# Small extra matmuls on TensorE after every step of the attention phase

## The reference

```
z   = q k^T / 8                              # per head, 2048 x 2048
lom = where(mask, -softplus(z), 0)           # mask: strictly lower triangle
s   = reverse_cumsum(lom, over keys) - lom
att = where(mask, exp(log_sigmoid(z) + s), 0)
o   = att v
x   = x + (o Wo^T) + moe_ffn(xn)             # 32 low-rank experts and a shared one
```

## Time and profile before

| | us |
|---|---|
| median of 3 runs (lowest, highest) | 8487.61 (8464.02, 8512.73) |
| the profiled execution: time | 8526.3 |
| its span, from the first to the last instruction (core 4, the slowest) | 8524.8 |
| spans of the 8 cores | 8405.2 to 8524.8 |
| mean granted TensorE clock of core 4 | 0.716 |
| PE busy, share of the span | 5427.3, 64% |
| DVE busy | 3253.1, 38% |
| ACT busy | 2889.5, 34% |
| weight loads of PE busy | 1589.4, 19% |

### The profile page before, as it was taken

How to read it: one execution, slowest core, us unless ns; L and a number is a source line. 1 busy time by engine, 2 the same in 40 slices (tenths; PEclk the granted TensorE clock), 3 DMA queues, 4 the chain that set the end, 5 groups by cost and what they waited for, 6 DMA issues and landing times.

```text
span 8524.8 us, 81563 instructions; the slowest of 8 cores (8405.2 to 8524.8 us)
## 1 busy us (share of the span) xinstructions
PE 5427.3 (64%) x17588; PEld 1589.4 (19%) x17588; DVE 3253.1 (38%) x5812; ACT 2889.5 (34%) x4306; POOL 854.9 (10%) x1617
## 2 busy tenths in 40 slices
PE   2223556677776777777677656377667757766775
PEld 0011111122211222222112112112222121222212
DVE  7211224344444444444444411166236506623650
ACT  0000334344444444444444500044125404512440
POOL 0101111110001111000010000100110010001001
PEclk9866655666655666666556578688888888878878
DMA  2001547510000000000000034311341161134116
GB/s 75 12 4 10 64 46 89 66 12 7 6 6 7 8 8 8 6 6 6 6 8 1 0 64 100 72 55 62 104 121 52 46 182 55 62 92 125 55 39 170
DMA packets 222122, 408.82 MB, mean 48 GB/s; under 512 B 141576, under 2 KB 144032, under 8 KB 215760
## 3 DMA queue, kind: packets, MB, share of 16 engines
q0 software_dynamic: 200592, 353.00, 19.5%
q1 hardware_dynamic: 20784, 50.47, 2.5%
q10 hardware_dynamic: 272, 0.14, 0.0%
HBM read 451.83 MB, written 85.07 MB: 63 GB/s over the span
## 4 chain that ended last, share of the span: by engine, by line
PE 45%; DMA 18%; DVE 13%; ACT 11%; issue 10%; another core or an unknown queue 2%; DVEq 1%; ACTq 0%; SPq 0%; POOL 0%; POOLq 0%
PE pbq L510 7%; PE zp L639 5%; PE zp L645 5%; DMA cd<-scr_cd 5%; ACT att L565 4%; DMA xp<-x 4%; PE pboA L579 4%; DVE gu L821 4%; PE zp L548 3%; DVE lsb L651 3%; PE pboB L579 2%; ACT g L813 2%; DMA wv<-WvT 2%; PE pbL L810 2%
## 5 line engine op out<-in xcount | busy, mean ns | idle before, releaser
L651 DVE TENSOR_TENSOR lsb<-zp,z 1x512 bf16<-1x512 f32 (+3 forms) x1152 | 668.7, 589 | 1324.8 <-PE zp L645 1309.1
L579 PE MATMUL pboA<-att,vtok 128*64 128x512 bf16 (+2 forms) x640 | 347.0, 542 | 885.8 <-ACT att L565 738.1
L606 ACT ACTIVATE texp<-zp 128x1024 bf16<-128x1024 f32 x448 | 458.8, 1024 | 912.8 <-PE zp L548 737.8
L565 ACT ACTIVATE att<-zp 128x1024 bf16<-128x1024 f32 x448 | 458.4, 1023 | 671.6 <-DVE lsb L651 432.3
L639 PE MATMUL zp<-sp,tri 128*128 128x512 bf16 (+3 forms) x1280 | 642.1, 508 | 55.6 <-DVE z L626 48.9
L626 DVE COPY z<-zp 1x512 f32<-1x512 f32 (+3 forms) x1152 | 623.9, 577 | 0.6 <-issue 0.2
L645 PE MATMUL zp<-lsb,ones 1*128 1x512 bf16 (+2 forms) x1152 | 611.0, 530 | 0.0
L821 DVE TENSOR_TENSOR gu<-g,pbL 128x512 bf16<-128x512 bf16 x704 | 484.1, 688 | 192.0 <-PE pboA L817 64.4
L821 DVE TENSOR_TENSOR gu<-g,zp 128x512 bf16<-128x512 bf16 x704 | 484.2, 688 | 169.8 <-PE zp L817 57.9
L793 ACT ACTIVATE zg<-zp 128x512 bf16<-128x512 f32 x64 | 38.2, 597 | 1488.2 <-PE zp L790 1488.2
L813 ACT ACTIVATE g<-zp 128x512 bf16<-128x512 f32 x704 | 420.6, 597 | 279.4 <-PE zp L807 204.3
(11 more groups left out here) (186 smaller groups left out, 6930.0 us busy)
## 6 DMA issues: line engine op xcount, KB each, us to landing
cd<-scr_cd POOLq DMA_DIRECT2D x256, 512.0 KB, 4.8
cgu<-scr_cgu POOLq DMA_DIRECT2D x136, 704.0 KB, 4.5
scr_cgu<-CguT POOLq DMA_DIRECT2D x32, 704.0 KB, 77.6
x<-x SPq DMA_DIRECT2D x16, 1024.0 KB, 4.8
scr_cd<-CdT POOLq DMA_DIRECT2D x32, 512.0 KB, 79.3
xp<-x SPq DMA_DIRECT2D x64, 256.0 KB, 4.8
out<-op SPq DMA_DIRECT2D x64, 256.0 KB, 3.0
out<-yst POOLq DMA_DIRECT2D x16, 1024.0 KB, 8.0
```

The lines of the kernel that those rows point to most:

```text
L565: Sc.op("ACT", lambda sc, zp=zp: sc.activation(t_att[zp][:], zpair_ap[zp][:], AF.Exp), reads=[pr[(0 if zp == 0 else 6)], pr[(0 if zp == 0 ...
L579: Sc.op("PE", lambda t, zp=zp, pjb=pjb, p0=p0, oc0=oc0, first=first, po=po, hs=hs: t.matmul(pbank[po][0:64, oc0:QT], t_vtok[:, pjb * 128 + ...
L651: Sc.op("DVE", lambda v, zp=zp, h0=h0, c0=c0, hs=hs: v.tensor_tensor(t_lsb[hs][:, c0:QT], zpair_ap[zp][0:1, h0 + c0:h0 + QT], t_z0[hs][:, ...
```

## The change

After every step of `gen_headpair`, and before the unit of `gen_qkv` that may follow it, PE issues three extra matmuls. Each multiplies a 64x64 corner of the constant tile tri with itself (64 rows, 64 weight columns, 64 moving columns) and writes the result to a corner of bank 4. Nobody reads it. The three are recorded as writers of bank 4, so the first of them is given a wait on whoever still reads that bank. It is 3 x 1984 = 5952 matmuls, each with its weight load; nothing is removed or moved.

```diff
@@ -21,6 +21,7 @@
 ATTN_HPS = None
+HEAT_N = 3
@@ -665,6 +666,13 @@
                     reads=[pr[po]], writes=[res("oF")])
             yield
 
+    def heat(n):
+        for _ in range(n):
+            Sc.op("PE", lambda t: t.matmul(
+                pbank[4][0:64, 0:64], t_tri[0:64, 0:64], t_tri[0:64, 0:64],
+                start=True, stop=True),
+                reads=[res("tri")], writes=[pr[4]])
+
     hps = list(range(NHC)) if ATTN_HPS is None else list(ATTN_HPS)
@@ -674,6 +682,7 @@
         for _ in gen_headpair(hp):
             step += 1
+            heat(HEAT_N)
             if nxt is not None and step % 2 == 0:
                 try:
                     next(nxt)
```

## The result

The changed kernel takes 8679.42 us (median of 10 runs, 8668.1 to 8753.28) against 8490.01 us (10 runs, 8447.14 to 8532.12). The ratio is 1.0236, with a 95% interval of 1.0203 to 1.027: slower by 2.4%. (The ratio is worked out over the runs; the quotient of the two medians is 1.0223.) The forecast was 8805 us, 3.7% slower, in a range of 8600 to 9060.

The account below looks back on a forecast made before the run. A serial ring of 5.77 us per key block in pure attention, at clock 0.50, bounds the kernel. 20.3 us for each of 15 pairs plus 12 us for the last make +316 us: 8805 us, range 8600 to 9060.

Parts of the forecast that it names:

- the ring: One key block's serial chain in pure attention, through PE, DVE, ACT and back to PE: 5.77 us, forecast about 6.1.
- the hole: PE's idle 2.05 us per key block, between the last L645 and the next pboA; forecast to shrink to about 1.4.
- (a): Groups after steps C and A, without projections: 0.66 us in PE's idle 2.05 us, so they cost nothing.
- (b): Groups after step B, without projections, on the serial chain: 30 x 0.33 = 9.9 us a pair (4.8 to 19.8).
- (c): Groups during projection units, where PE is full: 24 x 0.24 = 5.8 us a pair (1.9 to 11.5).
- L555's step: Nearest matmul, 128 weight and 128 moving columns: 0.22 us at clock 0.50, 0.16 at 1.00; half priced one extra matmul.
- (d): First extra matmul after a unit waits for DVE's evacuation of bank 4; with transposes 4.6 us a pair (4.1 to 5.5).
- (e): PE's clock: given nothing; the level stays at 0.50 in pure attention.
- R1: Rival: the fill brings the clock back in pure attention; -300 us, about 8190 us; chance 0.09.
- R2: Rival: no change, the group after step B vanishes too; time about 8520 us; chance 0.05.
- R3: Rival: waits on bank 4 drop the clock in the projection stage too; 96 us more, 8900 us; chance 0.08.
- the same length as before from the output projection on: Sign expected in the profile: everything from the output projection to the end keeps its length, no gain or loss.

Follow-up runs that it names:

- k12_after: The changed kernel run once more, unaltered; ratio 1.0239 (1.0164 to 1.0315) to the kernel before, attention 4331 us.
- k3_only_ac: The changed kernel with the three extra matmuls only after steps A and C, none after B; ratio 1.0108 to the kernel before, attention 4166 us.
- k0_before: The kernel before the change, run once more unaltered for a second profile; ratio 1.0025 (0.9989 to 1.0062), attention 4077 us.
- k1_bank2: The changed kernel with the extra matmuls writing bank 2, unused in attention, instead of bank 4; ratio 1.0193 to the kernel before, attention 4268 us.
- k10_dense6: Against the changed kernel: six full 128-row matmuls into bank 2, only after step C outside projection units; ratio 0.9489 to the kernel before.
- k4_dense4: Against the changed kernel: four full 128-row matmuls into bank 2, only after step C outside projection units; ratio 0.9594 to the kernel before.
- k6_dense4_64: Like the kernel with four full matmuls after step C, but on 64 rows instead of 128; ratio 1.0095 to the kernel before.

## Why the prediction was right, and where its sizes were off

The direction, the place and the mechanism held: serial work on the ring, nothing in the hole, a new wait on bank 4, no change of the clock. The sum was too large: 316 us forecast, 189 measured between the medians (222 between those of k12_after's runs and of the kernel before beside them, 8684.56 and 8462.33). Two things made it so: attention grew by 253 us and not by 316, and a later stage became shorter.

(a) Groups in the hole cost nothing: shown (the ring of k3_only_ac is 5.76 us, its last pair as long as that of k0_before).

(b) A group on the ring was put at 0.33 us (0.16 to 0.66): it is 0.29. (c) One at the fast clock at 0.24: it is 0.18 to 0.21. This pair of rows of the changed kernel at clock 1.00 shows a wait first, then the group, 3396.22 - 3396.04 = 0.18 us to the next start:

```profile
3396.04 0.25 PE L671 MATMUL pbq<-tri 64*64 64x64 bf16 x3 [0.50 <-DVE q L521]
3396.22 0.39 PE L640 MATMUL zp<-sp,tri 128*128 128x512 bf16 x1
```

Half of L555's step was a good price, a little high. With 0.29 and 0.20 the sum becomes 30 x 0.29 + 24 x 0.20 + 4.6 = 18.1 us a pair, 282 with the last, against 253 to 254 measured in attention. The comparison block by block says where the other 30 us are. Without the waits a pair grew by 12.1 us (k1_bank2) and not by 13.5; the waits add 4.1 and not 4.6; the last pair grew by 8.8 and not by 36 x 0.29 = 10.4. The term that is off is (c): the seven blocks with projection units grew by 2.5 to 3.1 us a pair in k1_bank2 (against k0_before and the first profile), not by 24 x 0.20 = 4.8. (c) had PE full there, and it wasn't throughout: in the block that closes the first query block PE waits 1.46 us a pair for att before the change and 0.74 us after it (core 4), so groups ran in idle time there too.

(d) The wait was forecast as 4.1 us a pair for the projection units, 62 us, and the trace has 31.3 + 16.9 + 14.1 = 62.3 us. That the two agree is luck. I had four waits of 1.02 us a pair, 60 in all, and none otherwise. The trace has three a pair directly behind a unit, 45 of 0.94 us, which are 42.4 us; the fourth unit after a C step is followed by the closing step with its product with v. The other 19.9 us are 60 shorter waits of 0.20 to 0.75 us that I had called hidden, such as the 0.50 above, in a block with no scores matmul behind the unit. The transposes wait 17.5 us, where I took 7.5 and a bound of 21. k1_bank2 gives back 63 to 72 us when it is gone.

(e) The clock stayed at 0.50 in pure attention and at 1.00 with projections, and R1 fell. R1's price was of the right kind: k10_dense6 has a ring of 4.29 us where I had said 5.77 - 1.5 = 4.3; what brought the clock was more work, on all rows. The rule of the Trainium skill, "TensorE: Matmul & The Clock Gate", section "What's actually happening", that activity releases the throttle, agrees with k4_dense4 (0.82) and is too coarse for k6_dense4_64, where PE is busy 95% of the time at 0.50. R2 is out by the same rows as (b). R3 came in a small way: of 176 projection units on each core (those after the first 900 us), 21 to 26 take over 0.26 us a matmul, a sign of the low level, against 20 or 21 before. At most six units of about 3 us each are under 20 us a core.

The term that was wrong is one that I set to nothing, "the same length as before from the output projection on". The output projection became 27 us shorter from k0_before to k12_after (329 to 302) and 54 shorter than in the profile that I had read (362 to 308). 253 - 54 = 199 us between the medians of the cores, near the 189 measured, and 254 - 27 = 227 for the repeats, near their 222. The total would lie in the range without this gain too; the gain only took it further from 8805. A gain there was in no part of my sum and in no rival.

## What to carry to other kernels

Filler matmuls must be priced by where they stand in the chain: six in a hole of 2 us were free, three on the ring cost their full 0.29 us, and a shared bank turned the harmless ones into waits of up to 0.9 us. If filler is to lift the clock, watch PEclk and not PE's busy time, put it into the hole, give it all 128 rows and an unused bank, and try several amounts: here two full matmuls did nothing, four won 4%, six 5%, and eight no more than six. Compare the stages that a change doesn't touch too, and take the profile of the unchanged kernel twice.

## What the runs showed of the hardware

- Four matmuls of 512 columns on 64 rows kept PE busy 189.72 of 200 us and the granted clock stayed 0.50; the same four on 128 rows brought it to 0.82 on average.
- A matmul with 64 weight columns and 64 moving ones, repeated, starts about every 0.06 us at clock 0.50 (six last 0.53 us and three 0.36 or 0.37, so about 0.17 for three more); the group of three costs 0.29 us in the list, more than three steps of 0.06, so entering and leaving the group costs about 0.1 us more. Whether that is the other tile shape or the weight load was not tried.
- The output projection, identical code, took 299 to 310 us in the changed kernel and 320 us or more in the kernel before, on all cores of two profiles each, for a reason that these runs didn't find.
